# Routed stage: seven expert masks formed once per chunk and kept on chip as bf16

## The reference

```
route = top-2 of softmax(x W_r)                      # 8 experts, once per token
repeat 2 times:                                      # "rounds" 0 and 1, same route
    h   = gelu([x, v] W1[e] + b1[e])                 # for each expert e, 64 wide
    ctl = sum over the two chosen e of w_e * (h W2[e] + b2[e]) + shared expert
    alpha, beta, gate = split(ctl)                   # sigmoid, softplus, sigmoid
    v = alpha*v - beta*(x - mu);  x = x + 0.1*gate*v # then a gated small MLP
```

## Time and profile before

| | |
|---|---|
| median of 3 runs | 893.38 us |
| the profiled execution's own time | 893.23 us |
| its span | 891.1 us |
| TensorE busy | 850.7 us (95%) |
| VectorE busy | 637.9 us (72%) |
| ScalarE busy | 549.5 us (62%) |
| GpSimd busy | 285.8 us (32%) |

### The profile page before, as it was taken

One profiled execution on the slowest core, in us unless ns is written; L12 is line 12 of the kernel. 1 busy time (PEld: TensorE's weight loads), 2 busy tenths in 40 slices (PEclk: granted clock), 3 DMA queues, 4 the chain that ended last, 5 costly groups with the idle time before them and its releaser, 6 DMA issues.

```text
span 891.1 us, 18124 instructions
## 1 busy us (share of the span) xinstructions
PE 850.7 (95%) x6222; PEld 589.5 (66%) x6222; DVE 637.9 (72%) x1597; ACT 549.5 (62%) x1538; POOL 285.8 (32%) x587
## 2 busy tenths in 40 slices
PE   8899999999999999999999999999999998999985
PEld 7688888888889877544444444444477765777652
DVE  5477777677776655677594675674989876889776
ACT  2566667767776776645535365345467678777553
POOL 4236544444555433100000000002146520334346
PEclk9899999999999999999999999999999999999899
DMA  8600000000000000000000000000000000000000
GB/s 344 138 1 2 1 1 2 1 2 1 2 1 2 1 1 1 1 1 0 1 0 1 0 1 1 0 1 1 1 27 2 3 2 1 3 2 3 13 14 24
DMA packets 7813, 13.42 MB, mean 15 GB/s; under 512 B 4342, under 2 KB 5036, under 8 KB 7468
## 3 DMA queue, kind: packets, MB, share of 16 engines
q1 hardware_dynamic: 7724, 12.27, 4.3%
HBM read 11.22 MB, written 1.05 MB: 14 GB/s over the span
## 4 chain that ended last, share of the span: by engine, by line
PE 66%; DVE 16%; POOL 8%; issue 5%; ACT 4%; DMA 0%; DVEq 0%; SPq 0%; POOLq 0%; ACTq 0%
PE psum L1528 10%; PE psum L766 6%; PE psum L806 4%; POOL rstd L514 3%; PE psum L749 3%; PE psum L758 3%; PE psum L1961 3%; PE psum L1943 2%; PE psum L834 2%; PE psum L2451 2%; POOL arena L1094 2%; PE psum L1537 2%; PE psum L1913 2%; DVE negmax L1004 2%; DVE arena L2047 2%
## 5 line engine op out<-in xcount | busy, mean ns | idle before, releaser
L511 POOL TENSOR_TENSOR ve<-mv,epsv 128x1 f32<-128x1 f32 x176 | 34.4, 196 | 475.3 <-DVE mv L506 475.3
L1528 PE MATMUL psum<-arena,w1f 128*128 128x512 f32 x240 | 109.5, 592 | 0.0
L514 POOL TENSOR_TENSOR rstd<-ve,epsv 128x1 f32<-128x1 f32 x176 | 99.8, 567 | 13.8
L904 ACT ACTIVATE arena<-psum,negmax 128x128 f32<-128x128 f32 x256 | 90.3, 405 | 22.2 <-DVE negmax L1004 22.2
L1528 PEld LDWEIGHTS psum<-arena,w1f 128*128 128x128 f32 x240 | 45.6, 190 | 49.6 <-issue 48.0
L1094 POOL TENSOR_TENSOR arena<-arena,rsum 128x512 f32<-128x512 f32 x64 | 65.2, 1039 | 7.0 <-DVE rsum L1010 7.0
L1004 DVE TENSOR_REDUCE negmax<-psum 128x8 f32<-128x1024 f32 x32 | 39.2, 1224 | 34.3 <-PE psum L806 34.2
L766 PE MATMUL psum<-arena 128*128 128x512 f32 x128 | 62.7, 612 | 0.3 <-ACT arena L973 0.2
L904 ACT ACTIVATION_READ_ACCUMULATOR arena<-psum,negmax 128x1 f32 x256 | 62.9, 246 | 0.0
L749 PE MATMUL psum<-arena,sclA 128*128 128x128 f32 x512 | 62.8, 276 | 0.1
L749 PEld LDWEIGHTS psum<-arena,sclA 128*128 128x128 f32 x512 | 60.1, 193 | 0.3 <-ACT arena L958 0.3
(11 more groups left out here) (356 smaller groups left out, 2025.7 us busy)
## 6 DMA issues: line engine op xcount, KB each, us to landing
w<-in_w0qk SPq DMA_DIRECT2D x2, 512.0 KB, 4.9
w<-in_w0vo SPq DMA_DIRECT2D x1, 1024.0 KB, 7.4
cT<-in_cT SPq DMA_DIRECT2D x1, 1024.0 KB, 14.7
out<-x_tok SPq DMA_DIRECT2D x4, 256.0 KB, 2.0
rows<-in_rows SPq DMA_DIRECT2D x1, 836.0 KB, 12.2
x_tok<-in_x_tok SPq DMA_DIRECT2D x1, 768.0 KB, 9.5
ctx_tok<-in_ctx_tok SPq DMA_DIRECT2D x1, 768.0 KB, 10.8
wa<-in_wa SPq DMA_DIRECT2D x1, 768.0 KB, 17.7
```

The source lines that it names most:

```text
L514: pool.tensor_tensor(rstd[:, u, self.i:self.i + 1], ve[:, u, self.i:self.i + 1], epsv[:, 1:2], ALU.pow) \
L904: m = nc.scalar.activation(e0[:, b, g, :], ps(k, P, j * P), ACT.Exp, bias=negmax0[:, b, g:g + 1], accum_out=sum0[:, b, g:g + 1])
L1528: nc.tensor.matmul(ps(k), w1("e2", j * 384 + arg * D, j * 384 + (arg + 1) * D), f1_Hm[:, n, 2 * j + i, :], start=False, stop=False)
```

## The change

In a first round TensorE forms the seven masks as before. ScalarE now copies each from PSUM to on-chip memory as bf16, waits for its own copy to end, and then posts one count (`f1_kept`). Its list gets the seven copies in the order of TensorE's `M` steps, in T0 among the late tiles' pieces. VectorE reads the mask there instead of in PSUM, and posts `f1_masked` instead of freeing a bank. In a second round TensorE forms no mask and ScalarE copies none; VectorE's seven products read the copies of the first round. Two sets of seven masks lie in memory that is idle in this stage, chunks 2 and 3 using those of 0 and 1 again. In a second round `att` moves behind H2 and `ou` behind Hs in TensorE's list. VectorE's list is unchanged.

```diff
@@ pe_turn (second round)
-                order += at("M", "A0") + at("M", "B0") + at("H", 2) + at("M", "A1") + at("M", "B1") + at("H", 3)
-                order += at("M", "A2") + at("M", "B2") + at("H", "s") + at("M", "AB")
+                order += at("H", 2) + at("H", 3) + at("H", "s")
@@ act_turn
+            if new[1] == 0:
+                order = first + (at("O") if new[0] else []) + at("H", 0) + at("H", 1) + at("M", "A0") + at("M", "B0") + at("H", 2) + at("M", "A1")
+                order += at("H", 3) + at("M", "B1") + at("H", "s") + at("M", "A2") + at("M", "B2") + at("M", "AB")
+            else:
+                order = at("H", 0) + at("H", 1) + at("H", 2) + at("H", 3) + at("H", "s")
@@ ACT_MIX (T0)
-                   front("l2", 10), front("lnt", 14), of_first("H", "s"), of_first("O"), ("R", 1, 0, None), front("h", 14), front("l1", 13),
-                   front("lnt", 15), front("l2", 11), front("h", 15), ...
+                   front("l2", 10), front("lnt", 14), of_first("H", "s"), of_first("O"), ("R", 1, 0, None), front("h", 14), of_first("M", "A0"), of_first("M", "B0"), front("l1", 13),
+                   of_first("M", "A1"), of_first("M", "B1"), front("lnt", 15), of_first("M", "A2"), front("l2", 11), of_first("M", "B2"),
+                   of_first("M", "AB"), front("h", 15), ...
@@ with_late
-            at = {"pe": [..., (("M", "B0"), "att", old), (("M", "A2"), "ou", old), ...
+            at = {"pe": [..., (("H", 2) if new[1] else ("M", "B0"), "att", old), (("H", "s") if new[1] else ("M", "A2"), "ou", old), ...
@@ f1_pe, B and X
-                            stored(pe, f1, f"m{it}{s}{j}", t)
+                            pe.wait_ge(f1_masked, masked(c, it, f"{s}{j}"))
@@ f1_act
+            if kind == "M":
+                k = take(f"m{it}{arg}")
+                if c >= 2 and arg == MASKS[0]:
+                    act.wait_ge(f1_masked, masked(c - 2, 1, MASKS[-1]))
+                nc.scalar.activation(f1_mask[n][MASKS.index(arg)], ps(k), ACT.Copy).then_inc(free[k], 1)
+                stored(act, f1, f"m{it}{arg}", t)
+                act.sem_inc(f1_kept, 1)
@@ f1_dve, M
-                filled(dve, f1, f"m{it}{arg}", t)
-                nc.vector.tensor_tensor(f1_Hm[:, n, MASKS.index(arg), :], f1_H[:, n, j, :], ps(k), ALU.mult).then_inc(free[k], 1)
+                if it == 0:
+                    dve.wait_ge(f1_kept, held(c, arg))
+                nc.vector.tensor_tensor(f1_Hm[:, n, i, :], f1_H[:, n, j, :], f1_mask[n][i], ALU.mult).then_inc(f1_masked, 1)
```

More of the change, by code:

```diff
@@ L1230, in act_turn @@
             first = [] if new[0] or new[1] else [("R", 0, 0, None)]
-            order = first + (at("O") if new[1] == 0 and new[0] else []) + at("H", 0) + at("H", 1) + at("H", 2) + at("H", 3) + at("H", "s")
-            order = order[:-2] + [("K", 0, 0, None)] + order[-2:] + [("R", 1, 0, None)] + at("O") + [("K", 1, 0, None)] if first else order
+            if new[1] == 0:
[3 more added lines that the diff above has]
+                order = at("H", 0) + at("H", 1) + at("H", 2) + at("H", 3) + at("H", "s")
             order += of("F") + ([("R", routed, 0, None)] if routed and not first else []) + at("C", BETA)
@@ L1383, in with_late @@
             of_old = next((x[1:3] for x in order if x[0] == "F"), (0, 0))
-            at = {"pe": [(("H", 1), "pt", old), (("M", "B0"), "att", old), (("M", "A2"), "ou", old), (("F", *of_old, None) if new[0] == 2 else ("B", BETA), "l2", old),
+            at = {"pe": [(("H", 1), "pt", old), (("H", 2) if new[1] else ("M", "B0"), "att", old), (("H", "s") if new[1] else ("M", "A2"), "ou", old), (("F", *of_old, None) if new[0] == 2 else ("B", BETA), "l2", old),
                          (("X", BETA), "qk", n), (("G", *of_old, None) if new[1] == 0 else ("B", GATE), "as", n)],
@@ L1453, in s1 @@
             return [sem(f"f1_{name}{n}") for n in range(2)]
-        f1_gap, f1_tanh, f1_onehot, f1_clamped, f1_exped, f1_log, f1_v, f1_xnext, f1_x = (
-            s1(x) for x in ("gap", "tanh", "onehot", "clamped", "exped", "log", "v", "xnext", "x"))
+        f1_gap, f1_tanh, f1_onehot, f1_clamped, f1_log, f1_v, f1_xnext, f1_x = (
+            s1(x) for x in ("gap", "tanh", "onehot", "clamped", "log", "v", "xnext", "x"))
         f1_chain = sem("f1_chain")
@@ L1472, in build, with masked, held @@
         F1_CLOCK = {('L', 0, 0, None): 4, ('H', 2, 0, 's'): 12, ('H', 3, 0, 's'): 8, ('F', 3, 1, None): 5, ('Z', 3, 1, None): 4}
+        f1_masked, f1_kept = sem("f1_masked"), sem("f1_kept")
+        spare = [arena[:, 16384:16896], mat(rows, ROWS, "f0_s1"), mat(rows, ROWS, "f0_s2"), ctx_tok[:, 1792:2048],
+                 f0w1[:, :], f0w2[:, :, :].rearrange("p c d -> p (c d)"), arena[:, 15360:16128]]
+        spare = [x[:, i * C1 // 2:(i + 1) * C1 // 2].bitcast(BF16) for x in spare for i in range(x.shape[1] // (C1 // 2))]
+        f1_mask = [spare[:len(MASKS)], spare[len(MASKS):]]
+        def masked(c, it, arg):
+            return len(MASKS) * [at for at, *_ in turns()].index((c, it)) + MASKS.index(arg) + 1
+        def held(c, arg):
+            return len(MASKS) * c + MASKS.index(arg) + 1
         def f1_pe(pe, x):
@@ L1516, in f1_pe @@
             if kind == "M":
-                if it == 0 and arg == MASKS[0]:
+                if arg == MASKS[0]:
                     stored(pe, f1, "oh", t)
@@ L1531, in f1_pe @@
                 if arg == BETA:
-                    stored(pe, f1, f"m{it}AB", t)
+                    pe.wait_ge(f1_masked, masked(c, it, "AB"))
                     stored(pe, f1, f"h{it}s", t)
@@ L1604, in f1_act @@
                 act.wait_ge(f1_clamped[n], nth(c, 2, it + 1))
-                nc.scalar.activation(f1_lb[:, n, :, :], f1_lb[:, n, :, :], ACT.Exp).then_inc(f1_exped[n], 1)
-                act.wait_ge(f1_exped[n], nth(c, 2, it + 1))
+                nc.scalar.activation(f1_lb[:, n, :, :], f1_lb[:, n, :, :], ACT.Exp).then_inc(f1_log[n], 1)
+                act.wait_ge(f1_log[n], nth(c, 4, 2 * it + 1))
                 nc.scalar.activation(f1_lb[:, n, :, :], f1_lb[:, n, :, :], ACT.Ln, bias=1.0).then_inc(f1_log[n], 1)
@@ L1675, in f1_dve @@
             if kind == "M":
-                k, j = f1.bank(f"m{it}{arg}", t), EC - 1 if arg == "AB" else int(arg[1])
+                i, j = MASKS.index(arg), EC - 1 if arg == "AB" else int(arg[1])
                 stored(dve, f1, f"h{it}{j}", t)
-                filled(dve, f1, f"m{it}{arg}", t)
-                nc.vector.tensor_tensor(f1_Hm[:, n, MASKS.index(arg), :], f1_H[:, n, j, :], ps(k), ALU.mult).then_inc(free[k], 1)
+                if it == 0:
+                    dve.wait_ge(f1_kept, held(c, arg))
+                nc.vector.tensor_tensor(f1_Hm[:, n, i, :], f1_H[:, n, j, :], f1_mask[n][i], ALU.mult).then_inc(f1_masked, 1)
             if kind == "err":
```

4 lines of the change are left out of this document (2 added, 2 removed).

## The result

| | before | after |
|---|---|---|
| median | 893.37 us (20 runs: one of 2140.85 us, the others 890.42 to 897.48) | 889.32 us (20 runs, 883.85 to 894.09) |
| profiled execution | 893.23 us | 884.22 us |
| its span | 891.1 us | 882.4 us |

The ratio of the medians is 0.9947 (0.9929 to 0.9965). The forecast was 887.0 us with a range of 884.5 to 891.0.

What follows compares the result with a forecast made beforehand. The prediction took TensorE, busy 95% of the span, as the bound nearly everywhere in the routed stage; its turn terms summed to -6.3 us from 893.23, 886.9, given as 887.0 us, range 884.5 to 891.0.

Steps and rivals of the forecast that it cites:

- T2: Second round: `ou` still starts when line 1079 allows, F follows some 0.3 us behind it; -2.1 us.
- T3: Second round: 1.54 us of masks and the 0.49 us wait before `att` go; -2.0 us.
- T6: Second round: seven masks go from TensorE and nothing else moves; -1.5 us.
- T4: First round: bank waits on VectorE go, but `ou` still waits for line 1079; 0 us.
- T0, order: First round: A0's late copy delays VectorE's product, then `apply1 13` and TensorE's `l1 13` behind it; +1.9 us.
- clock rival: T0: TensorE's idle gap after its fillers drops the clock, 1.7 us per stretch, 888.7 to 890.4 us; chance 0.2.
- One mask costs 0.22 us on TensorE: Routed stage: each mask takes TensorE 0.22 us, the seven of a turn 1.54 us.
- The cover before `clamp`: T2: VectorE waited 2.49 us before `clamp`, so 0.4 us remain after the shift and nothing is late.
- The copy at 0.65 us: First rounds: each ScalarE copy takes 0.60 us plus 0.05 for wait and post, 4.55 us a turn.
- the seconds are pinned too: VectorE's or ScalarE's chain holds F or `clamp`, so second rounds give less; 889.5 or 892.1 us; chance 0.13.
- T0 costs nothing: T0: A0's copy slips in earlier or later gaps take up the delay; 885.0 us; chance 0.09.
- ScalarE paces the masks: All four first rounds: copies on ScalarE hold VectorE and F; +10.0 us, 903 us; chance 0.05.

Runs made afterwards that it cites:

- Experiment 3: Changed kernel with chunk 0 (T0 and T2) back the old way: TensorE forms the masks in both rounds, VectorE reads them in PSUM; 886.98 us, ratio 0.9917.
- experiment 7: Changed kernel with ScalarE copying every mask twice, the second copy behind the end of the first; 888.77 us, ratio 0.9948.
- experiment 4: Changed kernel with 15 instead of 6 filler matmuls before `l1 13` in T0, the delayed order kept; 887.59 us, ratio 0.9942.
- Experiment 5: Changed kernel with its first rounds kept but the second rounds the old way, masks formed again and read in PSUM; 895.61 us, ratio 1.0019.
- experiment 6: Changed kernel with `att` and `ou` of second rounds moved forward, near their old places in TensorE's list; 891.68 us, ratio 0.9990.
- experiment 2: Changed kernel with `apply1 13` and `silu 14` moved ahead of the products waiting for ScalarE's copies in VectorE's T0 list; 882.76 us, ratio 0.9872.
- 8: Changed kernel with experiment 2's edit, and in T4 the late tile's `l2` behind B for beta and `R` behind `X`; 885.35 us, ratio 0.9922.
- 9: The kernel of experiment 2 run again unaltered; 885.19 us, ratio 0.9917.
- 11: The changed kernel run again unaltered for another profile; 888.69 us, ratio 0.9964.
- experiment 10: The changed kernel run again unaltered, for a trace at a low mean clock; 890.48 us, ratio 0.9957.

## Why the prediction was right, step by step

| step | predicted | measured | by |
|---|---|---|---|
| T2 | -2.1 | -2.14 | turns; 3 gives it back |
| T3 | -2.0 | -2.16 | turns |
| T5 | -1.1 | -1.12 | B of T4 to F of T5 |
| T6 | -1.5 | -1.94 | turns |
| T7 | -1.5 | -1.53 | turns |
| T1 | 0 | 0 | turns, 7 |
| T4 | 0 | +0.63 | F to B of T4 |
| T0, order | +1.9 | +2.05 | 4 |
| sum | -6.3 | -6.2 | |
| T0, clock | a rival | +1.4 | after against 4 |

The sum of the forecast held: experiment 4's stage, with the clock full, is 289.34 us, 6.19 under before. That it holds to 0.1 us is in part luck: T6, T3 and the small rest gave 0.7 us more than forecast, and T4 and T0's order took 0.8 us more. The range held too, but the median, 889.32 us, lies above the 885 to 888.5 of the likeliest case and inside the 888.7 to 890.4 of the clock rival. It is also above the 888.9 us that the prediction drew as the edge of "faster", to which it gave 0.69. And one of its own signs of being wrong appeared: T0 lost 3.5 us, more than 3, of which 2.05 are the order it had in its sum and the rest the clock.

The median is 2.3 us over the forecast, for two reasons that the prediction had not put into the likeliest case. The first is the rival *the clock falls in T0's gap*: it came true in all four profiles of the changed kernel, and in those of experiments 5, 6 and 7, which keep the gap; in the kernel before and in experiments 2, 3, 4, 8 and 9, whose gap is short or filled, T0's clock is 1.00. The condition was named (the gap after the twelve fillers, drawn from the earlier trace rows) and the price too, 1.7 us against about 1.4 measured, but it got a chance of 0.2 with T1's 1.00 as the argument against. That argument compared scattered idle time in T1 with one gap of 2.19 us; a single gap more than three times as long as any in the stage's rows (0.65 us at most) deserved more. The Trainium skill ("TensorE: Matmul & The Clock Gate", part 1) says of a kernel's start that how many matmuls run slow varies from run to run; here the fall in T0 came every time, and only its length varied, twice as long in experiments 7 and 11 as in the others. The second is the rest of the kernel, where the changed kernel's mean clock is lower in some runs: an estimated 0.8 us, which the prediction took as given from one profile. Only experiment 10 has the trace of such a run.

Step by step. *One mask costs 0.22 us on TensorE*: T7 has nothing else in it and gives 1.53 us for seven. *T2 is held by line 1079 and F follows at once*: F starts 0.30 us behind `ou`, and experiment 6 shows that the move of `ou` is what makes this possible. The cover before `clamp`, 2.49 us less 2.1 in the earlier trace rows, proved right as well: its wait in the kernel after is 0.33 us, so nothing was late, but T2 could hardly give more:

```profile
433.18 0.96 DVE L1714 TENSOR_SCALAR f_lb<-arena 128x1536 f32<-128x1536 f32 x1 [0.33 <-ACT arena L1620]
```

*T3*: -1.54 of masks and the 0.49 of `att` make 2.03, measured 2.16. *T6* gave 0.4 us more than its masks. One wait for a bank stood there that the prediction had not looked up, in the kernel before:

```profile
564.32 1.13 PE L1512 MATMUL psum<-lnT,w1f 128*128 128x512 f32 x2 [0.15 <-DVE arena L1679]
```

By the starts of the steps, the pair of masks ahead of it took 0.75 us where the other pairs of this turn took 0.43 and 0.44, and this product took 0.96 where the others took 0.86: 0.42 us in all. VectorE's products free no bank any more, and that wait went with them.

*T0, order*: predicted was that VectorE's product comes 1.7 us late, `l1 13` 1.75 and B 1.9. Measured against T0's first `H`, the product is 1.76 late (355.34 against 355.07, with T0 starting 1.49 earlier), `l1 13` 1.77, B 2.05 with the clock held. *The copy at 0.65 us*: it lasts 0.593, but two in a row are shown as 1.28, and A0's product starts 0.72 us after its copy: the wait for its own end and the post cost 0.1 rather than 0.05. It made no odds outside T0.

**The step of the sum that failed is "T4 likewise, 0".** It looked at `ou` and stopped there. After `ou`, GpSimd's two small operations (lines 511 and 514) feed `l2`, and these became slower though nothing of them changed (next section); TensorE's wait before `l2` grew from 0.61 to 1.24 us, and this is the +0.63. No run has T4's masks alone in PSUM, so this price is read from the chain of waits in the trace. The prediction followed each wait of TensorE in the routed stage to VectorE or ScalarE and never to GpSimd, so a change of its speed had no term in the sum.

Of the other rivals, *the seconds are pinned too* fell (8.9 us came from T2, T3, T5, T6 and T7 where 8.2 were forecast), *T0 costs nothing* fell, though experiment 2's one edit comes within 0.2 us of it, and *ScalarE paces the masks* fell by experiment 7.

What stays open: why runs of the changed kernel and its kin reach mean clocks of 0.978 to 0.982 and those of the kernel before none below 0.983. It isn't T0's gap alone, since experiments 3, 4 and 8, whose T0 holds its clock, had such runs too (1 of 6, 2 of 12 and 2 of 8). Only the place is shown, 740 to 890 us in experiment 10, not what there sets it off.

## What to carry to other kernels

When an engine with slack gets new work whose result another engine reads, look at what is queued behind the reader in its strict list: here, of the copies' 16.6 us on ScalarE, at most 0.2 us reached TensorE once the order was mended, while two operations queued behind the first products had cost 3.3 us with the clock that fell behind them. Work taken off the bound engine pays in full only if what waits for another engine is moved behind the rest of it (T2 and T3: 0.9 us without the move, 4.3 with it). And split the effect at the bound engine's own steps before comparing run times: these repeat to hundredths of a us wherever the clock holds, while run times spread over ten us with the clock.

## What the runs showed of the hardware

GpSimd's small operations last longer beside VectorE's product when both the product's operands are on chip, the first of them until the product's end. GpSimd's line 511 works on 128x1 elements; it runs while VectorE goes on with its products. In T4, before the change:

```profile
503.89 0.19 POOL L511 TENSOR_TENSOR ve<-mv,epsv 128x1 f32<-128x1 f32 x1 [41.90 <-DVE mv L506]
504.15 0.55 POOL L514 TENSOR_TENSOR rstd<-ve,epsv 128x1 f32<-128x1 f32 x1
```

and after it, with the product of VectorE beside the first and VectorE's wait for the second:

```profile
501.64 0.56 POOL L511 TENSOR_TENSOR ve<-mv,epsv 128x1 f32<-128x1 f32 x1 [39.05 <-DVE mv L506]
502.28 0.88 POOL L514 TENSOR_TENSOR rstd<-ve,epsv 128x1 f32<-128x1 f32 x1
```

```profile
501.48 0.67 DVE L1704 TENSOR_TENSOR arena<-arena,rows 128x512 f32<-128x512 f32 x1
...
503.26 0.34 DVE L520 TENSOR_SCALAR yln<-x_tok,mv,rstd 128x128 f32<-128x128 f32 x1 [0.52 <-POOL rstd L514]
```

The product ends at 502.15 and line 511 at 502.20. In every profile of the changed kernel and its kin where line 511 takes 0.54 to 0.56 us and the product is listed by itself, it ends 0.04 to 0.06 us behind that product; where no such product runs, it takes 0.19 (or up to 0.30 beside other operations). Experiment 3 tells the cause from the place, as its T2 reads the masks in PSUM and its T1, T3 and T4 on chip. GpSimd there:

```profile
389.84 0.56 POOL L511 TENSOR_TENSOR ve<-mv,epsv 128x1 f32<-128x1 f32 x1 [12.65 <-DVE mv L506]
...
422.03 0.19 POOL L511 TENSOR_TENSOR ve<-mv,epsv 128x1 f32<-128x1 f32 x1 [30.66 <-DVE mv L506]
...
461.09 0.55 POOL L511 TENSOR_TENSOR ve<-mv,epsv 128x1 f32<-128x1 f32 x1 [38.25 <-DVE mv L506]
...
501.66 0.56 POOL L511 TENSOR_TENSOR ve<-mv,epsv 128x1 f32<-128x1 f32 x1 [39.06 <-DVE mv L506]
```

Experiment 5 turns it around: 0.56 us in T1 and T4, its first rounds, 0.19 in T2 and T3. The operation is the same and so is VectorE's work beside it but for one operand, and where both are slowed they take 0.37 and 0.33 us longer. Five such pairs, in T0 to T4, make up 3.5 of the 3.8 us by which GpSimd is busier after the change. Experiment 7's T4 separates the two: there VectorE waits 0.33 us between its last two products. Line 511 takes 0.56 us beside the first of them; line 514 starts in that pause and is not slow, and the F to B step is 3.94 us instead of 4.11:

```profile
506.17 0.55 POOL L514 TENSOR_TENSOR rstd<-ve,epsv 128x1 f32<-128x1 f32 x1
```

One thing is left open: the mask on chip is also bf16 where the one in PSUM was float32, and no run keeps it on chip as float32, so place and type of the operand are not told apart.

The Trainium skill ("VectorE: DVE Perf Modes", "Two Vector instructions with no wait between them") names a second read interface for a VectorE instruction with two on-chip operands, shared with GpSimd. These rows agree with it, but show only the delay, not by what it comes about. VectorE's product pays nothing itself (682 against 678 ns).

TensorE's clock falls behind a single idle gap of 2.19 us in T0 (1.2 GHz for a piece, granted clock 0.93 over the stretch), and holds where the gap there is 0.18 or 0.43 us. It also holds behind the gap of 1.64 us in T1 of the kernel after:

```profile
389.39 0.46 PE L894 MATMUL psum<-wa,ctx_tok 128*128 128x128 f32 x2 [1.64 <-DVE ctx_tok L1079]
```

The granted clock of 363 to 636 us is 1.00 there, as in the row of experiment 10. The piece in T0 costs 1.3 to 1.5 us of the stage. The runs of this one program lie between 884 and 894 us with their mean clock, 0.992 to 0.978.
